# Row sums of half of the first attention's scores by a wide exponential, with the quantiser's rounding moved between engines

## The reference, cut to what matters

```python
def fake_quant(x, bits=8):                       # one scale for the whole tensor
    scale = jnp.maximum(jnp.max(jnp.abs(x)) / 127, 1e-08)
    return jnp.clip(jnp.round(x / scale), -128, 127) * scale

qkv = fake_quant(x) @ fake_quant(w_qkv) + b_qkv  # q, k, v: [B=32, H=12, N=128, hd=16]
attn = einsum('bhnd,bhmd->bhnm', fake_quant(q), fake_quant(k)) * hd ** -0.5
attn = fake_quant(softmax(attn, axis=-1))
out = einsum('bhnm,bhmd->bhnd', attn, fake_quant(v))
```

## Time and profile before

| what | value |
|---|---|
| median of 3 runs | 1969.83 us |
| the profiled execution's own time | 1969.73 us |
| its span, first to last instruction | 1968.1 us |
| busy share TensorE / VectorE / ScalarE / GpSimd | 79% / 66% / 49% / 24% |
| mean granted TensorE clock, share of full speed | 0.892 |

### The profile page before, as it was taken

One profiled execution on the slowest core, in us unless ns is written; L12 is line 12 of the kernel. 1 busy time (PEld: TensorE's weight loads), 2 busy tenths in 40 slices (PEclk: granted clock), 3 DMA queues, 4 the chain that ended last, 5 costly groups with the idle time before them and its releaser, 6 DMA issues.

```text
span 1968.1 us, 37567 instructions
## 1 busy us (share of the span) xinstructions
PE 1551.7 (79%) x13020; PEld 1205.5 (61%) x13020; DVE 1289.9 (66%) x4233; ACT 961.6 (49%) x2769; POOL 481.7 (24%) x689
## 2 busy tenths in 40 slices
PE   0076764888888758888888877999999949999996
PEld 0032221776666546666666656777777738888885
DVE  7898885787888767877877744666666642222221
ACT  1275999873545445554454423444444414444442
POOL 7401333000000012222222211222222223333332
PEclk9985555559999869999999988999999969999998
DMA  3000000119991000000000000000000038778785
GB/s 74 18 1 1 1 1 1 22 42 172 183 174 11 0 1 1 0 0 0 0 0 0 0 10 18 26 25 24 24 24 24 25 89 199 190 193 199 189 197 137
DMA packets 136263, 113.02 MB, mean 57 GB/s; under 512 B 29416, under 2 KB 128456, under 8 KB 136136
## 3 DMA queue, kind: packets, MB, share of 16 engines
q1 hardware_dynamic: 119320, 91.70, 20.3%
q0 software_dynamic: 16864, 20.33, 5.4%
HBM read 69.19 MB, written 45.94 MB: 59 GB/s over the span
## 4 chain that ended last, share of the span: by engine, by line
PE 46%; DVE 34%; ACT 12%; issue 4%; POOL 2%; DVEq 0%; DMA 0%; ACTq 0%; POOLq 0%; SPq 0%
ACT bank L716 9%; PE bank L2374 8%; PE bank L2364 6%; PE bank L1007 5%; PE bank L2359 3%; PE bank L1000 3%; PE bank L2030 2%; PE bank L1690 2%; DVE R L1577 2%; DVE WK L1577 2%; DVE R L1882 2%; PE bank L966 1%; PE bank L640 1%; PE bank L641 1%; PE bank L1718 1%
## 5 line engine op out<-in xcount | busy, mean ns | idle before, releaser
L1047 POOL TENSOR_TENSOR WK<-WK,mhalf 128x2 f32<-128x2 f32 (+1 forms) x96 | 78.7, 819 | 546.0 <-DVE WK L1024 247.1
L2411 ACT ACTIVATE R<-bank,R 128x256 f32<-128x256 f32 x234 | 98.5, 472 | 187.1 <-PE bank L2364 185.5
L716 ACT ACTIVATE bank<-bank,nbias,sc 128x128 f32<-128x128 f32 x384 | 168.9, 952 | 21.6 <-POOL nbias L528 21.6
L2291 POOL DMA_INDIRECT moe_sum<-WK x78 | 121.5, 1558 | 229.0 <-DMA moe_sum<-WK 166.2
L2262 DVE SCALAR_TENSOR_TENSOR WK<-bank,R,WK 128x192 f32<-128x192 f32 x78 | 28.9, 412 | 207.6 <-PE bank L2374 207.6
L716 ACT ACTIVATION_READ_ACCUMULATOR bank<-bank,nbias,sc 128x1 f32 x384 | 162.1, 726 | 0.0
L2374 PE MATMUL bank<-R 128*128 128x192 f32 x936 | 158.6, 326 | 0.0
L1007 PE MATMUL bank<-WK,R 96*128 96x256 f32 x576 | 147.5, 398 | 6.2 <-ACT WK L973 3.5
L2374 PEld LDWEIGHTS bank<-R 128*128 128x128 f32 x936 | 151.3, 190 | 0.1
L1007 PEld LDWEIGHTS bank<-WK,R 96*128 96x128 f32 x576 | 106.2, 194 | 25.9 <-ACT WK L973 6.6
L2364 PE MATMUL bank<-R 128*128 128x256 f32 x468 | 113.0, 392 | 0.0
(11 more groups left out here) (507 smaller groups left out, 4131.3 us busy)
## 6 DMA issues: line engine op xcount, KB each, us to landing
moe_rows_in<-zeros SPq DMA_DIRECT2D x1, 25026.0 KB, 147.2
R<-in_L_ffn_w SPq DMA_DIRECT2D x39, 576.0 KB, 5.0
R<-in_L_ffn_w SPq DMA_DIRECT2D x39, 384.0 KB, 3.1
R<-moe_rows_in SPq DMA_DIRECT2D x39, 194.0 KB, 4.6
R<-in_L_ffn_w SPq DMA_DIRECT2D x78, 96.0 KB, 3.7
R<-in_L_ffn_b SPq DMA_DIRECT2D x39, 96.0 KB, 5.1
moe_sum<-resid POOLq DMA_DIRECT2D x16, 192.0 KB
moe_sum<-WK POOLq DMA_INDIRECT x78, 5.9
```

The source lines that it names most:

```text
L716: ins = nc.scalar.activation(s, s, ACT.Exp, bias=nbias[:, u, k:k + 1], scale=col(SS), accum_out=units(sum_all, g, u)[:, k:k + 1])
L1047: nc.gpsimd.tensor_tensor(a.rs[:, 0:n], a.ve[:, 0:n], mhalf[:, 0:n], ALU.pow).then_inc(f.root, 1)
L2291: pool.indirect_dma_start(out=acc, out_offset=bass.IndirectOffsetOnAxis(ap=x_id[k % B3][:, t:t + 1].bitcast(U32), axis=0), in_=x_y[k % B3] ...
L2411: ins = nc.scalar.activation(x_hid[q], hidden_at(p, n), ACT.Gelu, bias=xb_1[h][:, q:q + 1])
```

## The change

Units are taken in pairs e (an even and the next odd one). The odd unit keeps its three exponentials with bias and accumulation. For the even unit, TensorE adds the negated maxima to the scores in the bank: a product of the f32 identity with the three maxima spread over 3 x 128 columns, accumulated onto the scores (`b_shift`). ScalarE then needs no bias per head and runs one exponential of 384 columns into `ex`, and VectorE sums it in rows (`row_sums`, `b_sum`). The q and k parts are taken out of PSUM by ScalarE (`taken`, `b_tq`) and rounded by GpSimd (`rounded`), both once VectorE's; VectorE keeps the values. GpSimd makes `nbias` for odd units only.

```diff
 (VectorE, part and turn_b)
-                nc.vector.tensor_scalar(tq[:, k - 2, :], bank[4 + k % 4][:, :], col((XWQ, XWK)[(k - 2) // 3]),
-                                        bqs[:, k - 2:k - 1], ALU.mult, ALU.add).then_inc(b_taken, 1)
-                v.wait_ge(b_taken, r + 1)
-                nc.vector.tensor_scalar(tokens(qk_all, n)[:, k - 2, :], tq[:, k - 2, :], MAGIC, MAGIC, ALU.add,
-                                        ALU.subtract).then_inc(b_qk, 1)
+            def row_sums(e):
+                v.wait_ge(b_exp, 2 * e + 1)
+                nc.vector.tensor_reduce(units(sum_all, e // 8, 2 * (e % 8)), ex[:, e % 4, :].rearrange("p (k n) -> p k n", k=3),
+                                        X, ALU.add).then_inc(b_sum, 1)
...
+                    if u % 2 and g + u > 1:
+                        row_sums(8 * g + u // 2 - 1)
 (GpSimd, pool_attn)
+            def rounded(r):
+                n, k = r // 8, r % 8
+                if k >= 2:
+                    pool.wait_ge(b_tq, 6 * n + k - 1)
+                    nc.gpsimd.tensor_scalar(tokens(qk_all, n)[:, k - 2, :], tq[:, k - 2, :], MAGIC, MAGIC, ALU.add,
+                                            ALU.subtract).then_inc(b_qk, 1)
+            for r in range(AHEAD):
+                rounded(r)
             for g in range(NG):
                 for u in range(16):
-                    pool.wait_ge(b_neg, 16 * g + u + 1)
-                    nc.gpsimd.tensor_scalar(nbias[:, u, :], units(neg_all, g, u), col(SS), None, ALU.mult).then_inc(b_bias, 1)
+                    if u % 2:
+                        pool.wait_ge(b_neg, 16 * g + u + 1)
+                        nc.gpsimd.tensor_scalar(nbias[:, u, :], units(neg_all, g, u), col(SS), None, ALU.mult).then_inc(b_bias, 1)
+                        if AHEAD + 8 * g + u // 2 < 8 * NG:
+                            rounded(AHEAD + 8 * g + u // 2)
                     if u in (7, 15):
                         with_bias(g, u // 8)
 (TensorE, tensor_attn)
                     mm.then_inc(b_sp, 1)
+                    if u % 2:
+                        pe.wait_ge(b_neg, 16 * g + u)
+                        nc.tensor.matmul(bank[(u - 1) % 4][:, 0:384].rearrange("p (k n) -> p k n", k=3), ident[:, :],
+                                         units(neg_all, g, u - 1).unsqueeze(2).to_broadcast([P, 3, P]), start=False, stop=True,
+                                         skip_group_check=True).then_inc(b_shift, 1)
 (ScalarE, scalar_attn)
+            def taken(r):
+                n, k = r // 8, r % 8
+                if k >= 2:
+                    act.wait_ge(b_p, r + 1)
+                    if n:
+                        act.wait_ge(b_qk, 6 * (n - 1) + k - 1)
+                    nc.scalar.activation(tq[:, k - 2, :], bank[4 + k % 4][:, :], ACT.Identity, bias=bqs[:, k - 2:k - 1],
+                                         scale=col((XWQ, XWK)[(k - 2) // 3])).then_inc(b_tq, 1)
+            for r in range(AHEAD):
+                taken(r)
             for g in range(NG):
                 for u in range(16):
-                    act.wait_ge(b_bias, 16 * g + u + 1)
+                    if u % 2 == 0:
+                        e = 8 * g + u // 2
+                        act.wait_ge(b_shift, e + 1)
+                        if e >= 4:
+                            act.wait_ge(b_sum, e - 3)
+                        nc.scalar.activation(ex[:, e % 4, :], bank[u % 4][:, 0:384], ACT.Exp, scale=col(SS)).then_inc(b_exp, 1)
+                        continue
+                    act.wait_ge(b_bias, 8 * g + u // 2 + 1)
                     for k in range(3):
...
                     ins.then_inc(b_exp, 1)
+                    if AHEAD + 8 * g + u // 2 < 8 * NG:
+                        taken(AHEAD + 8 * g + u // 2)
```

More of the change, by code:

```diff
@@ L283, in tower @@
             "a_xq", "a_xTp", "a_xT", "a_qkp", "a_qk", "a_top", "a_vp", "a_v")]
-        b_sc, b_p, b_taken, b_qk, b_vq, b_sp, b_neg, b_bias, b_exp, b_resid = [sem(n) for n in (
-            "b_sc", "b_p", "b_taken", "b_qk", "b_vq", "b_sp", "b_neg", "b_bias", "b_exp", "b_resid")]
+        b_sc, b_p, b_taken, b_qk, b_vq, b_sp, b_neg, b_bias, b_exp, b_resid, b_tq, b_shift, b_sum = [sem(n) for n in (
+            "b_sc", "b_p", "b_taken", "b_qk", "b_vq", "b_sp", "b_neg", "b_bias", "b_exp", "b_resid", "b_tq", "b_shift", "b_sum")]
         c_c, c_ln, c_pt, c_ptTp, c_ptT, c_sp, c_e, c_p, c_op, c_o = [sem(n) for n in (
@@ L404, in part @@
                 n, k = r // 8, r % 8
-                v.wait_ge(b_p, r + 1)
                 if k < 2:
+                    v.wait_ge(b_p, r + 1)
                     nc.vector.scalar_tensor_tensor(
@@ L410, in part @@
                     if k == 1:
-                        v.wait_ge(b_taken, r + 1)
+                        v.wait_ge(b_taken, 2 * n + 2)
                         if n:
@@ L415, in part @@
                         nc.vector.tensor_scalar(values(n), tv2, MAGIC, None, ALU.subtract).then_inc(b_vq, 1)
-                    return
-                if n:
-                    v.wait_ge(b_qk, 6 * (n - 1) + k - 1)
-                nc.vector.tensor_scalar(tq[:, k - 2, :], bank[4 + k % 4][:, :], col((XWQ, XWK)[(k - 2) // 3]),
-                                        bqs[:, k - 2:k - 1], ALU.mult, ALU.add).then_inc(b_taken, 1)
-                v.wait_ge(b_taken, r + 1)
-                nc.vector.tensor_scalar(tokens(qk_all, n)[:, k - 2, :], tq[:, k - 2, :], MAGIC, MAGIC, ALU.add,
-                                        ALU.subtract).then_inc(b_qk, 1)
+            def row_sums(e):
+                v.wait_ge(b_exp, 2 * e + 1)
+                nc.vector.tensor_reduce(units(sum_all, e // 8, 2 * (e % 8)), ex[:, e % 4, :].rearrange("p (k n) -> p k n", k=3),
+                                        X, ALU.add).then_inc(b_sum, 1)
             def reciprocals(g):
                 v.wait_ge(b_exp, 16 * (g + 1))
+                v.wait_ge(b_sum, 8 * (g + 1))
                 return nc.vector.reciprocal(rsum_all[:, 48 * g:48 * (g + 1)], sum_all[:, 48 * g:48 * (g + 1)])
@@ L446, in vector_attn @@
                 turn_b(g)
+            row_sums(8 * NG - 1)
             ch.step(reciprocals(NG - 1))
@@ L588, in part @@
                 n, k = r // 8, r % 8
-                if r >= 4:
-                    pe.wait_ge(b_taken, r - 3)
+                if r >= 4 and (r - 4) % 8 < 2:
+                    pe.wait_ge(b_taken, 2 * ((r - 4) // 8) + (r - 4) % 8 + 1)
+                elif r >= 4:
+                    pe.wait_ge(b_tq, 6 * ((r - 4) // 8) + (r - 4) % 8 - 1)
                 if k < 2:
@@ L611, in tensor_attn @@
                                               qk[32 * j:32 * j + 32, k, i * P:(i + 1) * P],
-                                              qk[32 * j:32 * j + 32, 3 + k, i * P:(i + 1) * P], start=True, stop=True)
+                                              qk[32 * j:32 * j + 32, 3 + k, i * P:(i + 1) * P], start=(u % 2 == 1 or k == 0),
+                                              stop=(u % 2 == 1), skip_group_check=True)
                     mm.then_inc(b_sp, 1)
+                    if u % 2:
[3 more added lines that the diff above has]
+                                         skip_group_check=True).then_inc(b_shift, 1)
                     if u % 2 == 0 and AHEAD + 8 * g + u // 2 < 8 * NG:
@@ L948, in tower @@
             a.n, a.bank = n, bank[4 * n:4 * n + 4]
-            a.sems = [sem(f"pair{n}_{i}") for i in range(36)]
+            a.sems = [(b_tq, b_shift, b_sum)[i - 21] if n == 0 and 21 <= i < 24 else sem(f"pair{n}_{i}") for i in range(35)]
             a.hs, a.x, a.xr, a.sq = take(M * D, M), take(M * D, M), take(M * D, M), take(M * D, M)
@@ L1051, in chain_over @@
             ch.clear()
-        F_ENDS, F_SEMS, L_STARTS, L_ENDS, L_SEMS, M_STARTS = 2, 21, 3, 4, 35, 5
+        F_ENDS, F_SEMS, L_STARTS, L_ENDS, L_SEMS, M_STARTS = 2, 24, 3, 4, 35, 5
         pe_cleared, act_cleared, pool_cleared = [sem(n + "_cleared") for n in ("pe", "act", "pool")]
```

## The result

The changed kernel takes 2054.48 us (median of 4 runs, 2050.78 to 2058.26) against 1971.35 us before in the same series: a ratio of 1.042, 95% interval 1.0402 to 1.0439. The direction was forecast; the size, 83 us where 16 were forecast, lies far outside the range.

A forecast was written before the change was run, and what follows sets the result against it. The prediction took a closed loop of waits between ScalarE and GpSimd to bound the pass: +20.0 us there, -3.6 before the loop, 0 after, net +16.4 on 1969.73, giving 1986 us; range 1976 to 2006.

The forecast's parts named there:

- The new wait: In the loop, ScalarE and GpSimd wait for each other from odd unit to odd unit: 3.29 us, against 2.64 a pair.
- the ring: The closed loop between ScalarE and GpSimd in pairs with a rounding, put at 3.29 us a turn.
- the sum: Seven groups at 24.8 us, including 1.0 for `with_bias`, and 15.2 for the eighth: pass 189.1 us against 169.1, +20.0.
- The rounding's price: GpSimd's rounding of a 512-column q or k part: 0.71 us each, 42 in the loop.
- the dearer slope: GpSimd's rounding at a two-input operation's 1.70 ns a column: 1.13 us each; as a rival 2004 us, chance 0.15.
- The shift's price: TensorE's 128 x 384 f32 product per pair: two passes, 0.32 us at 2.4 GHz or 0.64 at 1.2, plus 0.17.
- TensorE becomes the bound through the shift: Rival: the f32 product needs four passes at 1.2 GHz, 1.28 us, costing 11 us in short pairs: 1997 us, chance 0.05.
- long pairs: Pairs in the loop that the rival of four TensorE passes put at 2.97 us and still hidden.
- The last group: The loop's final eight pairs, without q, k or value parts: 1.9 us each, 15.2 us.
- The lead: Before the loop, ScalarE takes parts while GpSimd rounds: first exponential near 171.2 us instead of 174.79, -3.6.
- ScalarE's terms: In the loop, 384-column exponentials 0.49 us, takes 0.67 in a row or 0.78 alone; ScalarE's own sum 144 us.
- The paying rival: Rival: GpSimd finishes in time, ScalarE stays the bound at 2.48 us a pair: 1946 us, chance 0.05.

The follow-up runs named there:

- the run with both edits: The changed kernel with each rounding moved behind the next odd unit's scaled maxima on GpSimd and the shift made in bf16: 1963.52 us, ratio 0.9943.
- the first probe: The kernel before with seven single GpSimd operations ahead of its first score pass; 512-column two-operation roundings took 1.96 us to bf16, 1.91 to f32.
- the last version: The changed kernel with rounding back on VectorE one pair later, a bf16 shift one even unit later and the largest softmax value corrected: 1958.45 us, ratio 0.9919.

## Why the prediction was wrong

- **The new wait** was right in every link. The odd units are released by GpSimd's scaled maxima, 42 times, and one turn with the measured rounding comes to 4.52 us against 4.44 in the trace. Opening the ring alone, with every price left, gives 35 us back. The chain of waits of the changed kernel has the roundings 4.43 us apart, and 5.40 where `with_bias` stands between, the 1.0 more that the sum gave it:

```profile
189.38 1.93 POOL R L532
...
193.81 1.93 POOL R L532
...
199.21 1.93 POOL R L532
```

- **The rounding's price is the first step that failed**: "So 298 + 488 x 0.84 = 0.71 us, or 1.13 by the dearer slope". It measured 1.93. A fill's slope and a two-input operation's slope were used for a third kind of instruction, whose 24-column row gave only the constant. The real slope is 3.4 ns a column, four times the fill's and twice the two-input operation's; the bound at 1.13 was no bound. One turn of the ring was 1.2 us longer for it. With 1.93 in its place the prediction's own sum makes the pass 189.1 + 42 x 1.22 = 240.3 us, and 244.25 were measured: this one term is 51 of the 55 us by which the pass was off.
- **The shift's price is the second**: "Two passes of 384 columns at 2.4 GHz are 0.32 us". The 486 ns of the earlier trace rows are half a product. The trace writes each f32 product as two, and the rows could have told it: L1718 is issued once for each of 32 tiles, and the trace has two groups of 32 records for it (one stands in the earlier trace rows). The shift stands there 128 times for 64 issued, and holds TensorE for 1.58 us a pair where 0.81 was taken. The Trainium skill's FP8 and Floating Point Precision, section TensorE Precision Notes, gives four passes for true FP32. The trace agrees as far as it goes: the rival's four passes, 1.28 us, fit into the 1.58 us, and the bf16 product, one of them (0.32), holds TensorE for 0.43 (239.81 to 240.24 in the run with both edits). So the rival "TensorE becomes the bound through the shift" was right about the passes. Its 1997 us was too low, in part because its long pairs were put at 2.97 us; they measured 3.40: 0.86 for the six score products instead of 0.64, 0.96 for the part instead of 0.85, and 1.58 for the shift instead of 1.47.
- **The last group** is where the shift cost the changed kernel time of its own: 21.0 us (401.11 to 422.12) where 15.2 were forecast. With no part left, a second closed chain sets the pace, which the prediction does not have: the shift, the score products behind it, VectorE's maxima, the next shift. It takes 2.73 us a pair where 1.9 was taken:

```profile
402.15 1.65 PE bank L634 x2
403.79 0.44 PE bank L627 x6
...
404.26 0.57 DVE neg_all L432
...
404.87 1.65 PE bank L634 x2
```

- **The lead** went the other way: +3.1 instead of -3.6. It is the rounding's price again: six in a row take 12 us, 7.3 more than forecast, and the first score product waits for the last. The chain has them as one piece, and the timeline the wait:

```profile
162.34 11.97 POOL R L532 x6
...
174.36 0.50 PE L627 MATMUL bank<-R 32*128 32x128 bf16 x3 [7.98 <-POOL R L532]
```

- **ScalarE's terms held**: a 384-column exponential takes 0.48 us to the start of the next instruction (584 ns from its start to its end), a take 0.66 (778 ns), and its own sum was forecast at 144 us and is 145.9 busy when nothing else binds. The row sum was forecast at 0.55 and took 0.547, and VectorE's other work stayed hidden.
- **The paying rival** was right about what lies behind the ring once TensorE is out of the way too: 1946 us was its price, and 1958 is what a kernel reaches in which ScalarE is the bound again.

## What to carry to other kernels

Where two engines hand work to each other, write down each one's list for one period and look for a ring before pricing anything: the order of two instructions in GpSimd's list was worth 35 us here, and the slow rounding next to nothing once it stood behind the urgent one. Price an operation from a row of its own kind that is large in the dimension that grows; a small row gives the constant only. And count a row's records against the number of times its line is issued: where a product appears twice as often, one record is not its price.

## What had not been expected of the hardware

A TENSOR_SCALAR with two immediates on GpSimd takes some 0.21 us and 3.38 ns a column. At 512 columns it is 1.91 us into f32 and 1.96 into bf16 in the first probe, and 1.93 in the changed kernel's pass, where VectorE works about half of the time. A plain cast of 512 columns takes 0.92 us. VectorE does the same 512-column rounding in 0.43 us at the median and 0.49 on average in the last version. An f32 product stands in the trace as two records: 128 for the 64 shifts, 64 for the 32 products of L1718. The granted clock stayed at half through the whole pass in every version, also where TensorE was busy 199.0 of 209.4 us.
